# Causal masks added on TensorE: identity and mask tiles in F32R in place of BF16

## The chip, the cores and the metric
The kernel runs as one program on one core of a Trainium2 chip (trn2). The metric is the device time of one launch in microseconds (us); lower is better. A thousand nanoseconds (ns) are one us.

## The reference, cut to what matters
One transformer block for 2048 tokens of width 256: a ternary embedding, a layer norm, an attention of 16 heads with three branches (latent and window branches are causal, the select branch sees 64 chosen tokens), and a mixture of 8 experts.

```python
def _attn(q, k, v, causal):
    scale = 1.0 / math.sqrt(q.shape[-1])
    s = jnp.einsum('bhqd,bhkd->bhqk', q, k) * scale
    if causal:
        mask = jnp.tril(jnp.ones((Tq, Tk), dtype=bool))
        s = jnp.where(mask, s, jnp.finfo(s.dtype).min)
    return jnp.einsum('bhqk,bhkd->bhqd', jax.nn.softmax(s, axis=-1), v)
...
a1 = _attn(q, k1, v1, causal=True)     # latent
a2 = _attn(q, ks, vs, causal=False)    # select
a3 = _attn(q, kw, vw, causal=True)     # window
```

## The kernel before
The program runs in stages: `embed` (weights, tables, constants), `project`, `select`, `attend`, `mix`, `experts`. The change touches constants that `embed` makes, and products in `select` and `attend` that read them.

`attend` takes one head after the other, 16 in all. A head is cut into 84 units. A unit is one block of scores, keys (128 partitions) by up to 512 queries, of one branch. For unit i TensorE (PE) makes the scores with `pe_scores`, and four units later the product with the values with `pe_values`. All these operands are split into an upper and a lower F32R part, so the scores are three products (`three`: upper with upper on L1485, upper with lower on L1488, lower with upper on L1489) and the values two (upper part of the probabilities on L1575, lower on L1577). ScalarE (ACT) takes the exponentials (L1471, L1473), GpSimd (POOL) and VectorE (DVE) make the lower part of the probabilities (L1392). F32R is a 32-bit type that TensorE takes in one pass; the profile prints it as f32 on TensorE.

Between these, `pe_task` puts smaller tasks in the PE's stream, at places that a table (`schedule`) fixes:

- "max": a plain product of queries with keys (L1518), of which VectorE takes the row maxima (L1607). The maxima of the latent branch of this head and of the window branch of the next are made this way. For the select branch it is eight products of 64 columns (L1513).
- "prep": the projections for a later group of four heads (L1485 to L1489 on other tiles, and L1534). The last four heads have none.
- "neg": a transpose of the maxima (L1540).

The task results go to three PSUM banks in turn (`ps_x`, NX = 3), so task n waits until VectorE has read task n - 3.

Where a block of scores lies on the diagonal, the mask is added by a product of its own into the same PSUM bank: the identity is the stationary operand (lhsT) and a 128x128 mask with -1e30 above or below the diagonal is the moving one (rhs). In `pe_scores` this is L1559, between L1485 and L1488; in `pe_task` it is L1521, right behind L1518; in `select` L831, right behind L829. The block before the mask is 512, 384, 256 or 128 columns wide, each as often as the others. The trace writes `out<-moving,stationary`, and takes "ident" for ident16.

All engines run their own instruction streams in order, and the semaphores alone tie them together. The PE's weight loads (LDWEIGHTS, "PEld") are records of their own.

Of the kernel before, what the change touches and what calls it, by code (L numbers as in the profile page):

```python
# [10 lines left out]
F32 = mybir.dt.float32  # L11
F32R = mybir.dt.float32r
BF16 = mybir.dt.bfloat16
I32 = mybir.dt.int32
ALU = mybir.AluOpType
# [3 lines left out]
P = 128  # L19
# [12 lines left out]
MASKED = -1.0e30  # L32
# [57 lines left out]
def embed(nc, g, a, x, weight):  # L90
# [7 lines left out]
    with ExitStack() as ctx:  # L98
# [55 lines left out]
        @block.gpsimd  # L154
        def _(pool):
            pool.dma_start(idx[:], x.rearrange("o (t p) -> p (o t)", p=P)).then_inc(s["idx"], 16)
            cst = Count(pool, s["const"])
            cst.add(nc.gpsimd.memset(g.ones[:], 1.0))
            cst.add(nc.gpsimd.memset(g.ident[:], 0.0))
            cst.wait()  # L160
            cst.add(nc.gpsimd.affine_select(out=g.ident[:], in_=g.ident[:], compare_op=ALU.not_equal, fill=1.0,
                                            base=0, pattern=[[-1, P]], channel_multiplier=1))
            cst.wait()
            cst.add(nc.gpsimd.tensor_copy(g.ident16[:], g.ident[:]))

            cst.add(nc.gpsimd.memset(g.mask_qk[:], 0.0))
            cst.add(nc.gpsimd.memset(g.mask_kq[:], 0.0))
            cst.add(nc.gpsimd.memset(g.strict[:], 1.0))
            cst.add(nc.gpsimd.memset(g.ones16[:], 1.0))
            cst.add(nc.gpsimd.iota(g.slots[:], pattern=[[1, KEEP]], base=0, channel_multiplier=0, allow_small_or_imprecise_dtypes=True))  # L170
            cst.wait()
            cst.add(nc.gpsimd.affine_select(out=g.mask_qk[:], in_=g.mask_qk[:], compare_op=ALU.is_ge, fill=MASKED,
                                            base=0, pattern=[[-1, P]], channel_multiplier=1))
            cst.add(nc.gpsimd.affine_select(out=g.mask_kq[:], in_=g.mask_kq[:], compare_op=ALU.is_ge, fill=MASKED,
                                            base=0, pattern=[[1, P]], channel_multiplier=-1))
            cst.add(nc.gpsimd.affine_select(out=g.strict[:], in_=g.strict[:], compare_op=ALU.is_gt, fill=0.0,
                                            base=0, pattern=[[1, P]], channel_multiplier=-1))
            pool.wait_ge(s["idx"], 16)
            for t in range(NT):
                nc.gpsimd.indirect_dma_start(out=rows[:, t, :], out_offset=None, in_=weight,  # L180
                                             in_offset=bass.IndirectOffsetOnAxis(ap=idx[:, t:t + 1], axis=0)
                                             ).then_inc(s["gather"], 16)
            cst.wait()
            pool.wait_ge(s["wq"], 16 * (1 + KC))
            pool.wait_ge(s["w"], 16 * 6)
            nc.gpsimd.tensor_copy(g.wsm_hi[:], wsm[:]).then_inc(s["whi"], 1)
            nc.gpsimd.tensor_copy(g.wv_hi[:], wvw[:]).then_inc(s["whi"], 1)
            pool.wait_ge(s["whi"], 1)
            nc.gpsimd.tensor_tensor(g.wsm_lo[:], wsm[:], g.wsm_hi[:].bitcast(F32), ALU.subtract).then_inc(s["whi"], 1)
            pool.wait_ge(s["whi"], 2)  # L190
            nc.gpsimd.tensor_tensor(g.wv_lo[:], wvw[:], g.wv_hi[:].bitcast(F32), ALU.subtract).then_inc(s["whi"], 1)
            for n in range(NG):
                k = slot(n)
                if n == 3:
                    pool.wait_ge(wst[k], 32)
                kw = wkw[:, :, n, :]
                nc.gpsimd.tensor_copy(wq_s[k][:, 0, :], wq[:, n, :]).then_inc(s["ws"], 1)
                nc.gpsimd.tensor_copy(wkw_s[k][:, 0], kw).then_inc(s["ws"], 1)
                pool.wait_ge(s["ws"], 4 * n + 1)
                nc.gpsimd.tensor_tensor(wq_s[k][:, 1, :], wq[:, n, :], wq_s[k][:, 0, :].bitcast(F32), ALU.subtract).then_inc(s["ws"], 1)  # L200
                pool.wait_ge(s["ws"], 4 * n + 2)
                nc.gpsimd.tensor_tensor(wkw_s[k][:, 1], kw, wkw_s[k][:, 0].bitcast(F32), ALU.subtract).then_inc(s["ws"], 1)
            pool.wait_ge(s["ws"], 4 * NG)
            pool.wait_ge(s["whi"], 4)
# [532 lines left out]
def select(nc, g, a):  # L737

    with ExitStack() as ctx:
# [75 lines left out]
        @block.tensor  # L815
        def _(pe):
            done = 0

            def max_products(n, last):
                for t, c in maxima[n:last]:  # L820
                    b = bank[6 + n % 2]
                    if n >= 2:
                        pe.wait_ge(s["m_read"], n - 1)
                    if n == 0:
                        pe.wait_ge(s["q"], 48)
                        pe.wait_ge(s["kw"], 48)
                    w = min(CH, (t + 1) * P - c * CH)
                    diag = c == t // 4
                    ins = nc.tensor.matmul(b[:, 0:w], q_hi[0:DQK, t * P:(t + 1) * P], kw_hi[0:DQK, c * CH:c * CH + w], start=True, stop=not diag)  # L829
                    if diag:  # L830
                        ins = nc.tensor.matmul(b[:, w - P:w], g.ident16[:], g.mask_qk[:], start=False, stop=True)  # L831
                    ins.then_inc(s["m"], 1)
                    n += 1
                return n
            pe.wait_ge(s["flag"], 1)
            nc.tensor.matmul(bank[0][:, 0:NT], g.strict[:], flag[:], start=True, stop=False)
            pe.wait_ge(s["run"], 1)
            nc.tensor.matmul(bank[0][:, 0:NT], g.ones[:], run[:], start=False, stop=True).then_inc(s["pos"], 1)
            done = max_products(done, early)
            pe.wait_ge(s["hot"], 1)  # L840
            for kc in range(KC):
                for t in range(NT):
                    last = nc.tensor.matmul(bank[1 + kc][:, 0:KEEP], g.U[:, t, kc * P:(kc + 1) * P], hot[:, t, :], start=(t == 0), stop=(t == NT - 1))
            last.then_inc(s["sel"], 1)
            pe.wait_ge(s["w"], 32)
            pe.wait_ge(s["selc"], 1)
            for n in range(4):
                for kc in range(KC):
                    w = wk[:, kc, n * CH:(n + 1) * CH] if n < 3 else wv[:, kc, :]
                    last = nc.tensor.matmul(bank[(3, 4, 5, 2)[n]][0:KEEP, :], selT[:, kc, :], w, start=(kc == 0), stop=(kc == KC - 1))  # L850
                last.then_inc(s["ks"], 1)
                done = max_products(done, early + (n + 1) * (middle - early) // 4)
            pe.wait_ge(s["rope"], 1)
            for h in range(H):
                last = nc.tensor.transpose(bank[h // 8][0:DQK, (h % 8) * KEEP:(h % 8 + 1) * KEEP], krt[:, h, :], g.ident[0:KEEP, 0:KEEP])
            last.then_inc(s["kt"], 1)
            done = max_products(done, len(maxima))
            pe.wait_ge(s["khi"], 1)
            for n in range(2):
                pe.wait_ge(s["ks_read"], 3)  # L860
                for r in range(8):
                    last = nc.tensor.matmul(bank[3 + n][:, r * KEEP:(r + 1) * KEEP], q_hi[0:DQK, (8 * n + r) * P:(8 * n + r + 1) * P],
                                            khi[0:DQK, 0, 0:KEEP], start=True, stop=True)
                last.then_inc(s["m"], 1)
            pe.wait_ge(s["nm"], 1)
            nc.tensor.transpose(bank[5][0:2 * NT, 0:P], nm[:], g.ident[:]).then_inc(s["turn"], 1)
# [202 lines left out]
def attend(nc, g, a):  # L1069
# [7 lines left out]
    with ExitStack() as ctx:  # L1077
# [418 lines left out]
        def pe_task(pe, t):  # L1496

            n = XN[t]
            bank = ps_x[n % NX]
            if n >= NX:  # L1500
                pe.wait_ge(s["x_read"], n - NX + 1)
            if t[0] == "max":
# [12 lines left out]
                else:  # L1515
# [2 lines left out]
                    last = nc.tensor.matmul(bank[:, 0:w], q_hi[par][0:DQK, q * P:(q + 1) * P], k_hi[b][par][0:DQK, c * CH:c * CH + w],  # L1518
                                            start=True, stop=not diag)
                    if diag:  # L1520
                        last = nc.tensor.matmul(bank[:, w - P:w], g.ident16[:], g.mask_qk[:], start=False, stop=True)  # L1521
            elif t[0] == "prep":
                _, gr, what, j, part = t
                m = NJ * (gr - 1) + j
# [18 lines left out]
        def pe_scores(pe, h, i):  # L1543
# [12 lines left out]
            wait_unit(pe, "p_up", h, i - 3)  # L1556
            qs, ks = slice(j * CH + col, (j + 1) * CH), slice(k * P, (k + 1) * P)
            bank = ps_s[i % 3]
            mid = (lambda: nc.tensor.matmul(bank[:, col:col + P], g.ident16[:], g.mask_kq[:], start=False, stop=False)) if diag else None  # L1559
            aug = DQK + b + 1  # L1560
            three(bank[:, col:CH], k_hi[b][par][0:aug, ks], k_lo[b][par][:, ks], q_hi[par][0:aug, qs], q_lo[par][:, qs], mid, DQK).then_inc(s["scores"], 1)

# [738 lines left out]
def layer(nc, a, out):  # L2301
# [12 lines left out]
    with ExitStack() as ctx:  # L2314
        tile = lambda n, s, d=F32: ctx.enter_context(nc.sbuf_tensor(n, s, d))
        g.ident, g.ones = tile("ident", [P, P]), tile("ones", [P, P])
        g.ident16, g.mask_qk, g.mask_kq = tile("ident16", [P, P], BF16), tile("mask_qk", [P, P], BF16), tile("mask_kq", [P, P], BF16)
        g.gates, g.onehot, g.inv = tile("gates", [P, 3]), tile("onehot", [QA, NB]), tile("inv", [P, 1])
        with ExitStack() as mid:
            with ExitStack() as front:  # L2320
# [84 lines left out]
```

## Time and profile before

| | |
|---|---|
| median of 3 runs | 2747.41 us (2745.13 to 2747.56) |
| the profiled execution | 2745.16 us, span 2743.4 us |
| `attend`, first to last score product | 386.4 to 2312 us of the span |
| TensorE busy | 2327.9 us, 85% of the span |
| VectorE, ScalarE, GpSimd busy | 66%, 64%, 59% |

In the busy times, an instruction's duration runs from start to its modelled end, and two TensorE products that follow each other overlap. For TensorE the distance between the starts of two products is what counts, and it is read from the timeline, whose first column is the start in us and whose second is the duration.

### The profile page before, as it was taken

What the parts mean: (1) busy time and instruction counts of PE and PEld (TensorE: products, weight loads), DVE (VectorE), ACT (ScalarE), POOL (GpSimd) and SP (SyncE); (2) the same over time, 40 slices, a digit from 0 to 9 for tenths busy, and PEclk for the clock granted to TensorE, in tenths of its full rate; (3) what the DMA queues carried; (4) which work ended last, traced back from release to release, by engine and by line L of the source; (5) the groups of instructions that cost most, each with busy time, mean ns of one, the idle gap of its engine ahead of it and who ended that gap; (6) DMA issues with size and microseconds to landing.
All of it is one profiled execution on the core that took longest, in us unless ns stands there. A gap on an engine that the chain in (4) does not pass through costs nothing. (4 is left out here: it accounts for less than half of the span.)

```text
span 2743.4 us, 38402 instructions
## 1 busy us (share of the span) xinstructions
PE 2327.9 (85%) x12402; PEld 1845.8 (67%) x12402; DVE 1815.3 (66%) x2824; ACT 1743.7 (64%) x3574; POOL 1622.2 (59%) x1430
## 2 busy tenths in 40 slices
PE   0178579999999999999999999999999997538885
PEld 0155346777777777777777777777777775538885
DVE  2557457686776868687776868677686773455553
ACT  3433226777777777777777777777778776116663
POOL 4055316667676666767676666766656665006885
PEclk9985569999999999999999999999999998759998
DMA  9757654325151533414251533232132110615776
GB/s 382 311 187 246 189 127 108 91 68 136 24 154 29 136 66 108 112 48 124 52 142 38 138 69 91 61 67 60 34 67 49 32 25 17 194 62 177 197 203 169
DMA packets 199860, 314.87 MB, mean 115 GB/s; under 512 B 95915, under 2 KB 130219, under 8 KB 186731
## 3 DMA queue, kind: packets, MB, share of 16 engines
q1 hardware_dynamic: 189947, 298.23, 37.9%
q0 software_dynamic: 9712, 14.18, 2.8%
q8 instruction: 99, 1.62, 0.3%
q14 instruction: 102, 0.84, 0.1%
HBM read 210.20 MB, written 101.75 MB: 114 GB/s over the span
## 5 line engine op out<-in xcount | busy, mean ns | idle before, releaser
L1392 POOL TENSOR_TENSOR p_lo<-prob,p_hi 128x512 fp32r<-128x512 f32 (+2 forms) x960 | 1092.3, 1145 | 630.0 <-ACT p_hi L1473 544.7
L1471 ACT ACTIVATE prob<-ps_s 128x512 f32<-128x512 f32 (+4 forms) x1344 | 722.8, 538 | 465.8 <-PE ps_s L1489 303.0
L1607 DVE TENSOR_REDUCE max_part<-ps_x 128x1 f32<-128x128 f32 (+1 forms) x1240 | 713.4, 606 | 195.9 <-PE ps_x L1518 128.0
L1473 ACT ACTIVATE p_hi<-ps_s 128x512 fp32r<-128x512 f32 (+3 forms) x1344 | 718.5, 535 | 1.6
L1392 DVE TENSOR_TENSOR p_lo<-prob,p_hi 128x512 fp32r<-128x512 f32 (+1 forms) x320 | 308.0, 962 | 129.8 <-ACT p_hi L1473 124.4
L1575 PE MATMUL ps_o<-p_hi,v_win 128*128 128x512 f32 (+3 forms) x640 | 251.9, 394 | 8.5 <-DVE p_lo L1392 8.5
L1575 PE MATMUL ps_o<-p_hi,v_lat 128*128 128x512 f32 (+3 forms) x640 | 242.6, 379 | 0.0
L1577 PE MATMUL ps_o<-p_lo,v_win 128*128 128x512 f32 (+3 forms) x640 | 234.6, 367 | 0.0
L1577 PE MATMUL ps_o<-p_lo,v_lat 128*128 128x512 f32 (+3 forms) x640 | 234.1, 366 | 0.0
L1668 DVE TENSOR_TENSOR raw_o<-ps_o,low_sum 32x512 f32<-32x512 f32 x192 | 131.4, 684 | 78.9 <-ACT low_sum L1456 74.5
L1518 PE MATMUL ps_x<-k_hi,head_first 96*128 96x512 f32 (+2 forms) x320 | 120.6, 382 | 29.0 <-DVE max_part L1607 28.0
L1518 PE MATMUL ps_x<-k_hi,q_hi 96*128 96x512 f32 (+2 forms) x320 | 120.8, 383 | 26.7 <-DVE max_part L1607 26.0
L1575 PEld LDWEIGHTS ps_o<-p_hi,v_win 128*128 128x128 f32 x640 | 124.1, 194 | 27.3 <-DVE p_lo L1392 13.7
L1577 PEld LDWEIGHTS ps_o<-p_lo,v_lat 128*128 128x128 f32 x640 | 121.8, 190 | 19.6
L1575 PEld LDWEIGHTS ps_o<-p_hi,v_lat 128*128 128x128 f32 x640 | 122.2, 191 | 18.2 <-POOL p_lo L1392 0.3
L1577 PEld LDWEIGHTS ps_o<-p_lo,v_win 128*128 128x128 f32 x640 | 122.5, 191 | 16.8
L1485 PE MATMUL ps_s<-head_first 97*128 97x512 f32 (+1 forms) x320 | 123.5, 386 | 6.1 <-POOL v_lat L1408 6.0
L1488 PE MATMUL ps_s<-head_first 96*128 96x512 f32 (+1 forms) x320 | 128.1, 400 | 0.0
L2127 POOL DMA_INDIRECT xg<-x_scratch,slot_tok x46 | 51.5, 1120 | 128.6 <-POOLq L1723 118.0
L1488 PE MATMUL ps_s<-q_lo,kw_hi 96*128 96x512 f32 (+1 forms) x320 | 126.5, 395 | 0.0
L1488 PE MATMUL ps_s<-q_lo,k_hi 96*128 96x512 f32 (+1 forms) x320 | 126.1, 394 | 0.0
L1488 PE MATMUL ps_s<-head_first,k_hi 96*128 96x512 f32 (+1 forms) x320 | 126.1, 394 | 0.0
(432 smaller groups left out, 5830.9 us busy)
## 6 DMA issues: line engine op xcount, KB each, us to landing
raw<-in_experts_w_dram SPq DMA_DIRECT2D x23, 1536.0 KB
wbuf<-in_tok_weight_dram SPq DMA_DIRECT2D x16, 2000.0 KB, 16.9
head_first<-kw_scratch SPq DMA_DIRECT2D x72, 256.0 KB, 4.7
kw_scratch<-st_hi SPq DMA_DIRECT2D x48, 256.0 KB, 2.8
kw_scratch<-st_lo SPq DMA_DIRECT2D x48, 256.0 KB, 3.3
q_scratch<-st_hi SPq DMA_DIRECT2D x48, 256.0 KB, 4.8
q_scratch<-st_lo SPq DMA_DIRECT2D x48, 256.0 KB, 5.5
head_first<-q_scratch SPq DMA_DIRECT2D x48, 256.0 KB, 7.5
```

The lines of the kernel that those rows point to most:

```text
L1392: ns.tensor_tensor(upper if low else p_lo[:, i % LSLOTS, c:CH], prob[low:P, i % NPROB, c:CH], upper.bitcast(F32), ALU.subtract).then_inc(s ...
L1471: nc.scalar.activation(prob[low:P, i % NPROB, c:CH], ps_s[i % 3][low:P, c:CH], ACT.Exp, scale=SCALE).then_inc(s["p_full"], 1)
L1473: nc.scalar.activation(p_hi[:, i % SLOTS, c:CH], ps_s[i % 3][:, c:CH], ACT.Exp, scale=SCALE).then_inc(s["p_up"], 1)
L1485: nc.tensor.matmul(out, hi, xhi, start=True, stop=False)
L1488: nc.tensor.matmul(out, hi[0:rows] if rows else hi, xlo, start=False, stop=False)
L1518: last = nc.tensor.matmul(bank[:, 0:w], q_hi[par][0:DQK, q * P:(q + 1) * P], k_hi[b][par][0:DQK, c * CH:c * CH + w], start=True, stop=not ...
L1575: last = nc.tensor.matmul(bank[:, c:CH], w, p_hi[:, i % SLOTS, c:CH], start=(k == 0), stop=bool(low))
L1577: last = nc.tensor.matmul(bank[:, c:CH], w, p_lo[:, i % LSLOTS, c:CH], start=False, stop=output_of(i) is not None)
L1607: ins = nc.vector.tensor_reduce(mpart[:, q, c:c + 1], bank[:, 0:w], axis=AX.X, op=ALU.max)
L1668: nc.vector.tensor_tensor(raw_o[j * DV:(j + 1) * DV, h % 2, br, :], ps_o[BANK[out]][DV:2 * DV, :], low_sum[64 * (j % 2):64 * (j % 2) + DV, ...
L2127: nc.gpsimd.indirect_dma_start(out=xg[i % 2][:, q, :], out_offset=None, in_=g.x2_dram, in_offset=bass.IndirectOffsetOnAxis(ap=g.slot_tok[: ...
```

## The change
`ident16` becomes `ident_r`, and it and both masks are F32R in place of BF16. The GpSimd instructions that make them are the same ones on another type (a bitcast is only another view of the same bytes). The PE's stream has the same products in the same places; those on L831, L1521 and L1559 now read two F32R operands. The three tiles take 512 bytes in each partition in place of 256. The order of all instructions on all engines is unchanged.

```diff
@@ embed, gpsimd
-            cst.add(nc.gpsimd.tensor_copy(g.ident16[:], g.ident[:]))
-
-            cst.add(nc.gpsimd.memset(g.mask_qk[:], 0.0))
-            cst.add(nc.gpsimd.memset(g.mask_kq[:], 0.0))
+            cst.add(nc.gpsimd.tensor_copy(g.ident_r[:], g.ident[:]))
+
+            cst.add(nc.gpsimd.memset(g.mask_qk[:].bitcast(F32), 0.0))
+            cst.add(nc.gpsimd.memset(g.mask_kq[:].bitcast(F32), 0.0))
...
-            cst.add(nc.gpsimd.affine_select(out=g.mask_qk[:], in_=g.mask_qk[:], compare_op=ALU.is_ge, fill=MASKED,
+            cst.add(nc.gpsimd.affine_select(out=g.mask_qk[:], in_=g.mask_qk[:].bitcast(F32), compare_op=ALU.is_ge, fill=MASKED,
...
-            cst.add(nc.gpsimd.affine_select(out=g.mask_kq[:], in_=g.mask_kq[:], compare_op=ALU.is_ge, fill=MASKED,
+            cst.add(nc.gpsimd.affine_select(out=g.mask_kq[:], in_=g.mask_kq[:].bitcast(F32), compare_op=ALU.is_ge, fill=MASKED,
@@ select, tensor
-                        ins = nc.tensor.matmul(b[:, w - P:w], g.ident16[:], g.mask_qk[:], start=False, stop=True)
+                        ins = nc.tensor.matmul(b[:, w - P:w], g.ident_r[:], g.mask_qk[:], start=False, stop=True)
@@ attend, pe_task
-                        last = nc.tensor.matmul(bank[:, w - P:w], g.ident16[:], g.mask_qk[:], start=False, stop=True)
+                        last = nc.tensor.matmul(bank[:, w - P:w], g.ident_r[:], g.mask_qk[:], start=False, stop=True)
@@ attend, pe_scores
-            mid = (lambda: nc.tensor.matmul(bank[:, col:col + P], g.ident16[:], g.mask_kq[:], start=False, stop=False)) if diag else None
+            mid = (lambda: nc.tensor.matmul(bank[:, col:col + P], g.ident_r[:], g.mask_kq[:], start=False, stop=False)) if diag else None
@@ layer
-        g.ident16, g.mask_qk, g.mask_kq = tile("ident16", [P, P], BF16), tile("mask_qk", [P, P], BF16), tile("mask_kq", [P, P], BF16)
+        g.ident_r, g.mask_qk, g.mask_kq = (tile(n, [P, P], F32R) for n in ("ident_r", "mask_qk", "mask_kq"))
```

## Rows read from the trace of the kernel before

**Rows 1.** The page: busy us of each engine (share of the span)
```profile
PE 2327.9 (85%) x12402; PEld 1845.8 (67%) x12402; DVE 1815.3 (66%) x2824; ACT 1743.7 (64%) x3574; POOL 1622.2 (59%) x1430
```

**Rows 2.** Head 5 in three windows: length, busy by engine, TensorE's clock, DMA share, GB/s
```profile
1018.20:1030.00 11.80, 11.03 (x60) 8.44 (x59) 9.08 (x14) 8.73 (x19) 10.08 (x9) 1.00 1.02 229
1030.00:1064.20 34.20, 30.56 (x144) 22.41 (x143) 30.21 (x45) 23.64 (x47) 23.91 (x21) 1.00 0.56 170
1064.20:1131.80 67.60, 67.60 (x355) 53.55 (x354) 47.45 (x77) 52.02 (x107) 43.48 (x38) 1.00 0.09 21
```

**Rows 3.** TensorE's waits in head 5 (us in total, times, longest)
```profile
PE ps_x L1518 <- DVE max_part L1607: 3.7, 5, 1.3
```

**Rows 4.** Groups by line: the mask products (busy us, mean ns)
```profile
L1559 PE MATMUL ps_s<-mask_kq,ident 128*128 128x128 bf16 x512 | 119.1, 233 | 0.0
...
L1521 PE MATMUL ps_x<-mask_qk,ident 128*128 128x128 bf16 x496 | 114.9, 232 | 0.0
```

**Rows 5.** Timeline of TensorE, a mask in a block of 512 columns
```profile
1331.15 0.40 PE L1485 MATMUL ps_s<-q_hi,k_hi 99*128 99x512 f32 x1
1331.39 0.23 PE L1559 MATMUL ps_s<-mask_kq,ident 128*128 128x128 bf16 x1
1331.43 0.47 PE L1488 MATMUL ps_s<-q_lo,k_hi 96*128 96x512 f32 x1
1331.75 0.39 PE L1489 MATMUL ps_s<-q_hi,k_lo 96*128 96x512 f32 x1
```

**Rows 6.** Timeline of TensorE, ten products of 512 columns start between these two
```profile
1006.03 0.39 PE L1575 MATMUL ps_o<-p_hi,v_lat 128*128 128x512 f32 x1
...
1008.37 0.40 PE L1575 MATMUL ps_o<-p_hi,v_lat 128*128 128x512 f32 x1
```

**Rows 7.** Timeline of TensorE, a mask (left out) in a block of 256 columns
```profile
1336.65 0.28 PE L1485 MATMUL ps_s<-q_hi,k_hi 99*128 99x256 f32 x1
...
1337.01 0.28 PE L1489 MATMUL ps_s<-q_hi,k_lo 96*128 96x256 f32 x1
```

**Rows 8.** Timeline of TensorE, eight products of 64 columns, then 512
```profile
585.83 0.97 PE L1513 MATMUL ps_x<-ks_hi,head_first 96*128 96x64 f32 x8
586.64 0.48 PE L1575 MATMUL ps_o<-p_hi,v_win 128*128 128x512 f32 x1
586.95 0.40 PE L1577 MATMUL ps_o<-p_lo,v_win 128*128 128x512 f32 x1
```

**Rows 9.** Timeline of TensorE, two products of 128 columns after one of 512
```profile
1334.67 0.23 PE L1575 MATMUL ps_o<-p_hi,v_lat 128*128 128x128 f32 x1
1334.73 0.27 PE L1577 MATMUL ps_o<-p_lo,v_lat 128*128 128x128 f32 x1
1334.85 0.45 PE L1518 MATMUL ps_x<-head_first 96*128 96x512 f32 x1
```

**Rows 10.** Groups of weight loads, 560 to 2180 us (mean ns | idle before, what ended it)
```profile
L1489 PEld LDWEIGHTS ps_s<-head_first 96*128 96x128 f32 x280 | 53.5, 191 | 7.6
...
L1559 PEld LDWEIGHTS ps_s<-mask_kq,ident 128*128 128x128 bf16 x430 | 41.8, 97 | 67.5 <-issue 53.9
```

**Rows 11.** Timeline of TensorE, masks (left out) in blocks of 128 columns
```profile
1338.53 0.22 PE L1518 MATMUL ps_x<-head_first 96*128 96x128 f32 x1
...
1338.94 0.40 PE L1577 MATMUL ps_o<-p_lo,v_lat 128*128 128x512 f32 x1
1339.18 0.23 PE L1485 MATMUL ps_s<-q_hi,k_hi 99*128 99x128 f32 x1
...
1339.43 0.28 PE L1489 MATMUL ps_s<-q_hi,k_lo 96*128 96x128 f32 x1
```

**Rows 12.** Groups by line: GpSimd's gathers, and how it makes masks of either type
```profile
L180 POOL DMA_INDIRECT scratch<-in_tok_weight_dram,tok_idx x16 | 15.3, 959 | 8.7 <-issue 4.6 <-DMA tok_idx<-in_x_dram 4.2
...
L172 POOL TENSOR_SCALAR_AFFINE_SELECT mask_qk<-mask_qk 128x128 bf16<-128x128 bf16 x1 | 0.3, 292 | 0.1
...
L176 POOL TENSOR_SCALAR_AFFINE_SELECT strict<-strict 128x128 f32<-128x128 f32 x1 | 0.3, 286 | 0.0
```

## The prediction
> **What bounds the kernel now.** I read the page first: TensorE is busy for 85% of the span, no other engine for more than 66% [rows 1]. Then the windows of one head of the attention. In its last 67.6 us TensorE is busy for all 67.6 us, with VectorE at 47.45 and ScalarE at 52.02, and the clock is at its full level of 2.4 GHz, 1.00 [rows 2]. Here TensorE alone sets the pace: every ns that its stream gains or loses is a ns of the run. In the 46 us before, 1018.2 to 1064.2, TensorE is busy 41.59 us and VectorE 39.29 us [rows 2], and TensorE's waits, 3.7 us in five pieces, are all of one kind: a "max" product on L1518 waits for VectorE to have read the bank of three tasks ago [rows 3]. In this stretch a shorter TensorE stream mostly makes those waits longer. The order of the streams is unchanged, so what remains is the price of one mask product, and there are 512 on L1559 and 496 on L1521 [rows 4]; a quarter of each stand behind a block of 512, 384, 256 and 128 columns.
>
> **What a mask costs now.** The recorded durations (233 ns, rows 4) overlap with their neighbours, so I go by starts. From L1485 to L1489 of a diagonal block with 512 columns it is 1331.75 - 1331.15 = 0.60 us [rows 5]. Ten starts of 512-column products take 2.34 us, 0.234 each [rows 6], so that two of them would take 0.468, and the mask adds 0.132. With 256 columns the same distance is 0.36 [rows 7]; at half of 0.234 a product, two would take 0.234, and the mask adds 0.126. The mask itself starts L1488 only 0.04 us after it, but L1488 then lasts 0.47 and holds L1489 back to 0.32 [rows 5]: the wait is for L1488's weights, not for the mask's stream.
>
> **What an F32R product costs that is shorter than its weight load.** Eight F32R products of 64 columns and the start of the next take 0.81 us, and that next one, 512 wide, then takes 0.31 to the start behind it in place of 0.234 [rows 8]. Both come out of one rule: a product can't begin to stream until about 0.111 us after the one before began, because its weights load meanwhile. A record starts when the product before has finished streaming (64 columns: 0.03), so the first distance is 0.03 and seven are 0.111: 0.03 + 0.78 = 0.81. The last begins 0.111 - 0.03 = 0.08 after its record and streams 0.234: 0.31. Two 128-column F32R products say the same: the first distance is 0.06 (the stream), the second 0.12 [rows 9]. So F32R streams 128 columns in 0.06, at the same rate as 512, and no short block pays more than its weight load.
>
> **Why the BF16 mask costs 0.132 and not 0.111.** The weight load of an F32R product starts with the product before; that of the mask doesn't. Its group shows 53.9 us of idle time before it with no cause but "issue", for 430 loads [rows 10], where the loads of L1489 show none by that name. So now a mask pays some 0.02 for its own load, late and short, and then 0.111 for the load of the F32R product behind it.
>
> **The sum, by width.** I take it that the F32R mask is treated as the F32R products of rows 8 and 9 are.
> - Block of 512, 384 or 256 columns: the mask's load of 0.111 hides under the product before, which streams 0.117 or more. The mask starts on time, and the product behind it streams 0.111 later. The mask adds 0.111 in place of 0.126 to 0.132: -0.015 to -0.021, I take -0.018. There are 384 + 372 = 756 of them: -13.6 us.
> - Block of 128 columns: the product before streams only 0.06, so that the mask now waits for its own load too. On L1559, L1485 to L1489 is now 1339.43 - 1339.18 = 0.25 [rows 11] and becomes 0.06 + 0.111 + 0.111 = 0.282: +0.032, 128 times: +4.1 us. On L1521 with a 512-column product behind, it is now 1338.94 - 1338.53 = 0.41 [rows 11] and becomes 0.06 + 0.111 + (0.051 + 0.234) = 0.456: +0.045 by this instance, 124 times. The narrow block pays for the same wait as on L1559, and a timeline gives a difference to no better than 0.01, so between +0.032 and +0.045 I take +0.037: +4.6 us.
>
> All masks of the attention: -13.6 + 4.1 + 4.6 = -4.9 us, about -0.31 a head. How much of it counts: by a count in the timeline of head 5, 22 of its 64 masks start in the stretch from 1018.2 to 1064.2. By width they are 8 on L1559 (two of each) and 14 on L1521 (four each of 128 and 256, three each of 512 and 384), which comes to 16 x -0.018 + 2 x 0.032 + 4 x 0.037 = -0.076 us. If all of that disappears in VectorE's waits, a head is left with -0.23 and the run with -3.7 us; if none, -4.9. The last four heads have no prep tasks and fewer such waits. I take -4 us. Against the profiled execution (2745.16) this is 2741; that execution is 2.25 us below the median of the runs, and against the median the forecast is 2747.4 - 4 = 2743.4 us.
>
> **The rest of the edit at nothing.** GpSimd makes a mask in 292 ns as BF16 and in 286 as F32 [rows 12], and afterwards it waits 4.2 us for the token indices before the gathers on L180 [rows 12], which covers some 0.1 us either way. Without that cover it would be 0.1 us. The 16 masks of `select` (L831) at some 0.02 to 0.1 each are between -0.4 and +1 us. The larger tiles move the addresses of those behind them; no row prices that, and I take nothing, with a bound of 1 us either way.
>
> **A rule against the change.** Rows 10 show 97 ns for a BF16 load and 191 for an F32R one. The Trainium skill, "TensorE: Matmul & The Clock Gate", section "Weight-path perf modes — Fast Weight Load (FWL) and DoubleRow", says that a full 128-column load that isn't FP32 is read in a faster mode with four chunks at once, and that FP32 gains nothing there. The trace agrees as to the order of the two. By that page alone the change gives up a faster load on every mask, and the estimate from its P / 1.2 ns for a plain load is 107 ns against a quarter of it, 80 ns more for each of 1008 masks, or +81 us. This is a price only where the load is exposed.
>
> **Rivals.**
> 1. *The mask's load stays exposed* (slower). The idle time before the mask's load could come from something other than its type: from the identity being reused, or from a product that adds into the bank that is being written. Then the F32R load of 0.111 stands open before each mask, and the mask adds 0.111 + 0.111 = 0.222 in place of 0.132: +0.09 each. Times 1008 that is +91 us, or with the 22 of 64 masks in the VectorE-bound stretch counted at nothing, +60: 2807 to 2838 us. It decides from the point where the load is late by more than 0.02. Against it: L1488 adds into the bank that L1485 writes and its load is early. For it: no row shows this load in F32R. 6%.
> 2. *The 128-column blocks lose nothing* (clearly faster). If the load of the identity could start before the product in front of it, or were shorter, only the -0.018 would be left, times 1008: -18 us, 2729. Rows 8 and 9 speak against it, with 128 stationary columns in each. 7%.
> 3. *Nothing measurable, gain and loss cancel.* If a third of the 0.018 belongs to the short product and not to its type, the wide masks give 756 x -0.012 = -9.1, the narrow ones +8.7: 2747. 25%.
> 4. *The losses weigh more.* If an F32R mask behind a wide product is no cheaper at all (the late load was hidden too, and 0.132 is what any short product costs there), the narrow ones stand alone: +8.7 us, less the VectorE-bound part, 2753 to 2756. Rows 8 speak against it (0.31 in place of 0.32 behind the short product). 10%.
> 5. The forecast above, from -2 to -7 us: 52%.
>
> **How the numbers follow.** The likeliest is 2743.4 us, its own range 2740 to 2746. The range for 8 in 10 takes rivals 3 and part of 4 in and leaves 1 and most of 2 out: 2733 to 2751. What a measurement of this kernel can tell from no change is about 0.2%, 5.5 us. The forecast's range reaches over that line with a third of its weight or somewhat more, 0.20 of 0.52; with rival 2 and a little of rival 3 that is 0.30 for faster. Slower is rivals 1 and most of 4, 0.13. The rest, 0.57, is no change.
>
> **What would show it.** In the changed profile the loads on L1559 and L1521 should last about 190 ns and have no "issue" before them; from L1485 to L1489 it should be 0.58 us with 512 columns (0.60 now), 0.345 with 256 (0.36) and 0.28 with 128 (0.25). The three windows of rows 2, 113.6 us together, should become 113.4. If the load still starts with the mask and L1485 to L1489 takes 0.69, rival 1 holds. If L1559 shows a distance of more than 0.06 to the next start behind a wide block, an F32R mask streams more slowly than rows 9 let expect, and the sum is wrong there.

## The result and the profile after

The changed kernel takes 2751.01 us (median of 16 runs) against 2746.15 us before (16 runs): ratio 1.0025, 95% interval 1.0016 to 1.0035. That is slower and not 4 us faster: by some 7 us going by the ratio and the means of the 16 runs (2752.5 against 2745.4), by 4.9 us going by the medians. The range of the prediction ended at 2751.0. Ratios leave out two executions in the runs further down, one of run 4 (3343 us) and one of the kernel before beside runs 5, 8, 9 and 11 (3344 us), which had a granted clock of 0.65 where all others have 0.93.

The profiled execution of the changed kernel took 2754.81 us, with a span of 2753.1 us. Of the 9.6 us between the two profiled spans, 0.5 lie ahead of the attention, 2.6 in its first head and 0.3 behind the last. The first head has no weight in this: over the thirteen kernels profiled here it took from 126.5 to 137.7 us, in no order by kernel. What is left, 6.3 us, comes from heads 1 to 15: 5.4 from heads 1 to 14 and 0.9 from the last. Up to head 14 it is regular: heads 1 to 11 take 122.81 us (from the first L1485 of one to that of the next) where they took 122.39, all but head 10, which takes 122.23; heads 12 to 14, which have no prep tasks, take 0.44 to 0.47 us more than before.

**The products themselves.** The timeline of TensorE in the changed kernel, a mask behind blocks of 512, 256 and 128 columns:

```profile
1091.57 0.40 PE L1485 MATMUL ps_s<-q_hi,k_hi 99*128 99x512 f32 x1
1091.81 0.22 PE L1559 MATMUL ps_s<-mask_kq,ident_r 128*128 128x128 f32 x1
1091.87 0.44 PE L1488 MATMUL ps_s<-q_lo,k_hi 96*128 96x512 f32 x1
1092.15 0.39 PE L1489 MATMUL ps_s<-q_hi,k_lo 96*128 96x512 f32 x1
...
1017.33 0.29 PE L1485 MATMUL ps_s<-q_hi,kw_hi 97*128 97x256 f32 x1
...
1017.69 0.28 PE L1489 MATMUL ps_s<-q_hi,head_first 96*128 96x256 f32 x1
...
1018.28 0.23 PE L1485 MATMUL ps_s<-q_hi,kw_hi 97*128 97x128 f32 x1
1018.34 0.27 PE L1559 MATMUL ps_s<-mask_kq,ident_r 128*128 128x128 f32 x1
1018.45 0.27 PE L1488 MATMUL ps_s<-q_lo,kw_hi 96*128 96x128 f32 x1
1018.56 0.28 PE L1489 MATMUL ps_s<-q_hi,head_first 96*128 96x128 f32 x1
```

The rows show 0.58 us from L1485 to L1489 with 512 columns, where [rows 5] have 0.60, and 0.28 with 128, where [rows 11] have 0.25. The mask streams for 0.06 us and L1488 for 0.28 behind it; behind the narrow block the distances are 0.06, 0.11 and 0.11. This is the model of the prediction to within 0.01 us. The medians over all such blocks of heads 2 to 14 (start distances, 104 of each) are 0.576, 0.468, 0.352 and 0.285 us for 512, 384, 256 and 128 columns, and in the kernel before 0.598, 0.484, 0.367 and 0.249.

The weight loads, as groups in the stretch 560 to 2180 us:

```profile
L1559 PEld LDWEIGHTS ps_s<-mask_kq,ident_r 128*128 128x128 f32 x428 | 81.5, 190 | 13.4
L1521 PEld LDWEIGHTS ps_x<-mask_qk,ident_r 128*128 128x128 f32 x429 | 81.1, 189 | 11.9
```

They last 190 ns in place of 97 [rows 10], and the idle time "issue" in front of them is gone. The load of the mask at 1091.81 starts at 1091.57, with L1485; in [rows 5] it starts with its own product, at 1331.39.

**Where the time went.** TensorE's waits from 600 to 2200 us. First the changed kernel, then the kernel before:

```profile
PE ps_x L1518 <- DVE max_part L1607: 42.7, 59, 1.4
PE ps_o L1575 <- DVE p_lo L1392: 7.6, 13, 0.6
PE ps_x L1540 <- DVE neg_max L1611: 5.0, 12, 0.4
```

```profile
PE ps_x L1518 <- DVE max_part L1607: 42.6, 59, 1.3
PE ps_o L1575 <- DVE p_lo L1392: 7.5, 13, 0.6
```

A wait stands there that wasn't there before: the transpose of the negated row maxima (L1540, unit 40 of a head) waits for VectorE's L1611, 0.42 us as a record, once a head. The same place in the timeline of the changed kernel, head 5, TensorE, VectorE and GpSimd:

```profile
1078.44 0.40 PE L1489 MATMUL ps_s<-q_hi,head_first 96*128 96x512 f32 x1
1079.26 0.27 PE L1540 MATMUL ps_x<-ident,neg_max 128*16 128x128 f32 x1 [0.42 <-DVE neg_max L1611]
...
1075.69 1.30 POOL L1392 TENSOR_TENSOR p_lo<-prob,p_hi 128x512 fp32r<-128x512 f32 x1 [0.17 <-ACT p_hi L1473]
1075.72 1.82 DVE L1691 TENSOR_TENSOR raw_o<-raw_o 128x512 f32<-128x512 f32 x1
1077.57 1.29 DVE L1607 TENSOR_REDUCE max_part<-ps_x 128x1 f32<-128x512 f32 x2
1078.89 0.22 DVE L1611 TENSOR_REDUCE neg_max<-max_part 128x16 f32<-128x64 f32 x1
```

and of the kernel before:

```profile
1070.98 0.69 DVE L1691 TENSOR_TENSOR raw_o<-raw_o 128x512 f32<-128x512 f32 x1
1071.00 1.81 POOL L1392 TENSOR_TENSOR p_lo<-prob,p_hi 128x512 fp32r<-128x512 f32 x1 [0.22 <-ACT p_hi L1473]
```

L1691 is the last addition of the three branches' outputs of the head before, which VectorE does in unit 35. It lasts 1.82 us in place of 0.69, and GpSimd's subtraction of unit 36 lasts 1.30 in place of 1.81. Before, VectorE starts 0.02 us ahead of GpSimd; after, GpSimd starts 0.03 us ahead. Whoever is first runs at its own length, and the other lasts 1.12 us (VectorE) or 0.5 us (GpSimd) longer. VectorE is then 1.12 us late for L1607 and L1611. L1489 to L1540 takes 0.82 us in place of 0.233, so TensorE stands for 0.58 us of it; the other 0.54 it had in hand. (The 0.42 of the record is the idle time from the end of L1489's record, which is 0.40 long and would overlap the next one.) Head 10, where GpSimd comes 0.19 us behind VectorE in both kernels, has no such wait, and it alone is shorter than before.

### The profile page after: what moved, and what is told of

Same layout as the page of the kernel before. It is cut to its first block and busy times, and to the rows that moved or that the text cites. A ratio compares the mean times of both kernels' runs of the same rounds, so it can differ in the third digit from the quotient of the medians.

```text
span 2753.1 us, 38402 instructions
## 1 busy us (share of the span) xinstructions
PE 2335.7 (85%) x12402; PEld 1963.3 (71%) x12402; DVE 1838.7 (67%) x2824; ACT 1744.1 (63%) x3574; POOL 1607.8 (58%) x1430
## 5 line engine op out<-in xcount | busy, mean ns | idle before, releaser
L1392 POOL TENSOR_TENSOR p_lo<-prob,p_hi 128x512 fp32r<-128x512 f32 (+2 forms) x960 | 1080.3, 1134 | 650.9 <-ACT p_hi L1473 566.0
L1607 DVE TENSOR_REDUCE max_part<-ps_x 128x1 f32<-128x128 f32 (+1 forms) x1240 | 714.7, 606 | 196.6 <-PE ps_x L1518 126.7
L1575 PE MATMUL ps_o<-p_hi,v_win 128*128 128x512 f32 (+3 forms) x640 | 246.3, 385 | 8.7 <-DVE p_lo L1392 8.7
L1575 PE MATMUL ps_o<-p_hi,v_lat 128*128 128x512 f32 (+3 forms) x640 | 239.5, 374 | 0.0
L1575 PEld LDWEIGHTS ps_o<-p_hi,v_win 128*128 128x128 f32 x640 | 122.2, 191 | 28.1 <-DVE p_lo L1392 13.9
L1575 PEld LDWEIGHTS ps_o<-p_hi,v_lat 128*128 128x128 f32 x640 | 120.9, 189 | 18.6 <-POOL p_lo L1392 0.3
L1485 PE MATMUL ps_s<-head_first 97*128 97x512 f32 (+1 forms) x320 | 122.8, 384 | 6.3 <-POOL v_lat L1408 6.0
L1488 PE MATMUL ps_s<-head_first 96*128 96x512 f32 (+1 forms) x320 | 124.6, 389 | 0.0
L1488 PE MATMUL ps_s<-q_lo,kw_hi 96*128 96x512 f32 (+1 forms) x320 | 122.2, 382 | 0.0
L1488 PE MATMUL ps_s<-q_lo,k_hi 96*128 96x512 f32 (+1 forms) x320 | 122.0, 381 | 0.0
L1488 PE MATMUL ps_s<-head_first,k_hi 96*128 96x512 f32 (+1 forms) x320 | 122.0, 381 | 0.0
```

The lines of the kernel that those rows point to most:

```text
L1392: ns.tensor_tensor(upper if low else p_lo[:, i % LSLOTS, c:CH], prob[low:P, i % NPROB, c:CH], upper.bitcast(F32), ALU.subtract).then_inc(s ...
L1485: nc.tensor.matmul(out, hi, xhi, start=True, stop=False)
L1488: nc.tensor.matmul(out, hi[0:rows] if rows else hi, xlo, start=False, stop=False)
L1575: last = nc.tensor.matmul(bank[:, c:CH], w, p_hi[:, i % SLOTS, c:CH], start=(k == 0), stop=bool(low))
L1607: ins = nc.vector.tensor_reduce(mpart[:, q, c:c + 1], bank[:, 0:w], axis=AX.X, op=ALU.max)
```

## The experiments

Theory A: the F32R masks shorten TensorE's stream as forecast, but bring GpSimd's subtraction forward past VectorE's addition, and the 0.58 us wait a head comes from that. Theory B: F32R masks themselves cost time. A head below is the median length of heads 1 to 11 in the profiled execution. Most heads of a profile repeat to some 0.1 us or better, so this is the finer measure; the ratio of whole runs carries the unsteady first head. Every ratio is to the kernel before.

**1. VectorE late by a memset, BF16 masks.**

```diff
                 if br == 2:
                     dve.wait_ge(s["done"], 2 * h + 1)
+                    nc.vector.memset(tick[:, 0:32], 0.0)
```

> The kernel before (BF16 masks) with one added VectorE memset of 128x32 in front of the last addition of each head's output (L1691, third branch), so that this addition starts some 0.05 to 0.15 us later. Theory A (the changed kernel is slower because the addition now starts just behind GpSimd's subtraction of unit 36 in place of just ahead of it): the addition lasts 1.8 us in place of 0.69, the transpose L1540 waits about 0.6 us, a head takes 122.9 to 123.0 us in place of 122.4, and the run is 7 to 10 us slower (ratio 1.0025 to 1.0035) with not one F32R mask in it. Theory B (the F32R masks themselves cost the time, in TensorE's stream or its clock): no change, within 1 us.

Measured: ratio 0.9996 (0.9984 to 1.0008), head 122.37, the addition 0.65 us. The two engines in head 5:

```profile
1069.58 1.81 POOL L1393 TENSOR_TENSOR p_lo<-prob,p_hi 128x512 fp32r<-128x512 f32 x1 [0.22 <-ACT p_hi L1474]
1069.60 0.09 DVE L1692 MEMSET tick<- 128x32 f32 x1
1069.60 0.66 DVE L1693 TENSOR_TENSOR raw_o<-raw_o 128x512 f32<-128x512 f32 x1
```

As theory B had it, but the edit didn't do what it was for. By the record starts the addition is now 6 to 19 ns behind GpSimd (15 in head 5, all heads but head 10), and yet it is GpSimd that waited (1.81 us). So the outcome of the pair did not flip, and this run tells nothing between A and B. Why VectorE stayed the first isn't shown. It does show that the order of two record starts this close is not always the order that counts. Run 5 makes the delay in another way.

**2. GpSimd late, F32R masks.** One more instruction on GpSimd, behind the waits of unit 36 and in front of its subtraction.

```diff
+            if i == 36:
+                nc.gpsimd.memset(tick[:], 0.0)
```

> The changed kernel (F32R masks) with one added GpSimd memset of 128x128 between the waits and the subtraction of unit 36, so that this subtraction starts some 0.14 us later and VectorE's addition is ahead of it again. Theory A: the addition is back at 0.69 us, L1540 waits for nothing, a head takes 122.2 us, and the run is 2 to 4 us faster than the kernel before (ratio 0.9985 to 0.9993), 8 to 10 faster than the changed one. Theory B: as slow as the changed kernel, ratio 1.0025.

Measured: ratio 0.9984 (0.9971 to 0.9998), head 122.23. All additions are short again (the source line of the addition; least, median and greatest ns of the 32):

```profile
L1694 DVE TENSOR_TENSOR raw_o<-raw_o x32: 683/692/693, 574.2 to 2324.5; 128x512 f32<-128x512 f32 x32
```

With an instruction more than the changed kernel, this one is faster by more than 0.5 us a head. Theory B falls as the cause of the slowdown.

**3 and 4. The addition moved out of the way, with F32R and with BF16 masks.**

```diff
-        FINISH = {20: 0, 27: 1, 29: 2, 31: 3, 33: 4, 35: 5}
+        FINISH = {20: 0, 27: 1, 29: 2, 31: 3, 33: 4, 37: 5}
```

> The changed kernel with the last step of the output (L1691, third branch) moved from unit 35 to unit 37, behind the last row maximum and its negation L1611. Theory A: the addition finds GpSimd idle (between its units 36 and 39) and stays near 0.69 us, and the transpose no longer hangs on it in any case: no wait on L1540, a head of 122.2 us, ratio to the kernel before 0.998 to 0.9993. Theory B: ratio 1.0025.

> The kernel before with the same move of the last step to unit 37. Theory A: TensorE had no wait there, so nothing is won: ratio 0.9995 to 1.0003, a head of 122.4 us. With after_fin37 it then gives what the F32R masks are worth alone: my sum says 3 to 5 us in the whole run.

Measured: with F32R 0.9985 (0.9971 to 1.0000), head 122.23; with BF16 0.9995 (0.9981 to 1.0008), head 122.41. Without the collision the F32R masks are worth 0.18 us a head, some 2.8 us in 16 heads. That is the sign of the forecast, and less than its 4 us. But it doesn't come from where the forecast had it. The sum of the prediction, cut by units, against the medians of heads 1 to 11 from run 4 to run 3:

| stretch of a head | length | masks wide, narrow | forecast | measured |
|---|---|---|---|---|
| units 0 to 6 | 8.7 us | 4, 1 | -0.04 | -0.03 |
| units 7 to 32, the waits for VectorE | 46.0 us | 16, 6 | 0, at most -0.08 | -0.06 |
| units 33 to 40 | 10.5 us | 4, 0 | -0.07 | -0.11 |
| units 41 to 83, TensorE alone | 57.2 us | 24, 9 | -0.12 | +0.02 |

So the whole gain is made ahead of unit 41. Behind it, taken from the start of the product in front of a mask to the start of the second one behind it, the 24 wide masks gain 0.345 us, 0.014 each, and the nine narrow ones lose 0.35: 0.034 to 0.039 each, and 0.10 for two that stand next to each other. The two cancel, but for 0.02.

**5. VectorE late by a read of PSUM, BF16 masks.** `longer` is true for the last row maximum of unit 35.

```diff
+                    if longer:
+                        nc.vector.tensor_reduce(tick[:, 8 * h + q % 8:8 * h + q % 8 + 1], bank[:, 0:32], axis=AX.X, op=ALU.max)
                     ins = nc.vector.tensor_reduce(mpart[:, q, c:c + 1], bank[:, 0:w], axis=AX.X, op=ALU.max)
```

> The kernel before (BF16 masks) with one added VectorE row maximum of 32 columns of a PSUM bank, into a tile that nobody reads, once a head in unit 35, so that the addition L1691 of the third branch starts about 0.1 us later and behind GpSimd's subtraction of unit 36. It reads PSUM, where the memset of the run before_dve_late wrote SBUF and was itself ahead of GpSimd. Theory A (which of the two starts first decides): the addition lasts 1.7 to 1.8 us in place of 0.69, GpSimd's subtraction 1.3 in place of 1.8, L1540 waits 0.5 to 0.7 us, a head takes 122.9 to 123.1 in place of 122.4, the run is 7 to 10 us slower than the kernel before (ratio 1.0025 to 1.0037). Theory B (the F32R masks cost the time by themselves): 0.1 us a head at most, ratio 1.0000 to 1.0006.

Measured: ratio 1.0024 (1.0013 to 1.0035), head 122.87. The timeline of VectorE:

```profile
1071.97 0.18 DVE L1609 TENSOR_REDUCE tick<-ps_x 128x1 f32<-128x32 f32 x1
1072.07 0.68 DVE L1610 TENSOR_REDUCE max_part<-ps_x 128x1 f32<-128x512 f32 x1
1072.78 0.69 DVE L1671 TENSOR_TENSOR raw_o<-ps_o,low_sum 32x512 f32<-32x512 f32 x1
1073.50 1.77 DVE L1694 TENSOR_TENSOR raw_o<-raw_o 128x512 f32<-128x512 f32 x1
```

The added instruction puts VectorE 0.10 us back. The addition is then 0.07 us behind GpSimd and lasts 1.77 us, and L1540 waits 0.35 us as a record, less than expected. The head is 0.48 us longer than before and the ratio that of the changed kernel: the whole slowdown, without one F32R mask.

**6 and 7. Half of the masks.** F32R for L1559 alone, and for L1521 alone; the select stage stays BF16.

> F32R masks only in the score blocks (L1559, mask_kq); those of the row maxima (L1521) and of the select stage stay BF16; order of the steps as before. Behind TensorE's last wait for VectorE in a head (unit 32) exactly one mask of each kind runs before ScalarE releases GpSimd's subtraction of unit 36 (both in unit 34, both behind 384 columns). Each moves that subtraction 0.02 us forward against the addition L1691, from 0.02 behind it to level with it; both moved it to 0.03 ahead. Theory A: level is too close to call; if the addition wins (0.69 us) a head is 122.3 us and the ratio 0.999, if it loses (1.8 us) a head is 122.9 us and the ratio 1.0025. Either way duration and head go together. Without theory A a head should be half of the change's way in both runs.

> The other half: F32R masks only in the row maxima (L1521), BF16 in the score blocks. The same expectation: one mask in unit 34 moves GpSimd's subtraction 0.02 us forward, level with the addition; 122.3 us a head and a ratio of 0.999 where the addition stays at 0.69, 122.9 and 1.0025 where it lasts 1.8.

Measured: L1559 alone 1.0016 (1.0005 to 1.0027), head 122.77, GpSimd 0.011 to 0.020 us ahead (a shift of about 0.04 us and not the expected 0.02), and all additions but that of head 10 long. L1521 alone 0.9997 (0.9987 to 1.0006), and here the heads of one execution fall apart. VectorE and GpSimd in head 1, then in head 2:

```profile
581.94 1.84 DVE L1698 TENSOR_TENSOR raw_o<-raw_o 128x512 f32<-128x512 f32 x1
...
581.93 1.30 POOL L1399 TENSOR_TENSOR p_lo<-prob,p_hi 128x512 fp32r<-128x512 f32 x1 [0.19 <-ACT p_hi L1480]
...
704.75 0.69 DVE L1698 TENSOR_TENSOR raw_o<-raw_o 128x512 f32<-128x512 f32 x1
...
704.75 1.84 POOL L1399 TENSOR_TENSOR p_lo<-prob,p_hi 128x512 fp32r<-128x512 f32 x1 [0.20 <-ACT p_hi L1480]
```

Of heads 1 to 14, the five in which GpSimd starts 6 to 9 ns ahead have an addition of 1.83 us (and those of the first twelve heads take 122.79 to 122.84 us). The eight in which the distance is between 2 ns ahead and 1 ns behind, and head 10 with 185 ns behind, have one of 0.69 us (122.23 to 122.25). Up to the start of unit 40 the eleven heads agree to 0.03 us (63.82 to 63.85); from there they take 58.97 to 58.99 with a long addition and 58.40 with a short one. So duration and head go together, in one execution of one kernel, as theory A has it.

**8. F32R only behind the narrow blocks.** Order of the steps as before.

> The mirror image: F32R masks only behind blocks of 128 columns, BF16 behind the others, order of the steps as before. By my sum each narrow mask costs 0.032 (L1559) or 0.037 us (L1521), 8 of each a head, less those in VectorE's stretch: +0.35 to +0.55 us a head (122.75 to 122.9), +6 to +8 us in the run by TensorE's stream alone. Theory A also says that TensorE and ScalarE are then later and not earlier against VectorE, so that the addition L1691 stays ahead of GpSimd (0.69 us) and L1540 doesn't wait.

Measured: ratio 1.0027 (1.0015 to 1.0040), head 122.69, or +0.30; the additions last 0.69 us and L1540 doesn't wait. The mechanism is as expected; the size is below the expected 0.35 to 0.55. The heads account for some 5 us of the 7.5 that the ratio gives. The profiled execution (2747.68 us) is 5.8 us below the median of its runs, and where the rest is stays open.

**9, 10 and 11. F32R only behind the wide blocks,** with the addition in unit 37, with it in unit 35, and with the first multiplication (L1685; in the kernel before it lasts 1.78 us in heads 1 to 15, 1.65 in head 8) moved as well. The choice is made where the product is issued:

```diff
-    g.ident_r[:], g.mask_qk[:]
+    (g.ident16 if w == P else g.ident_r)[:], (g.mask_qk16 if w == P else g.mask_qk)[:]
...
-    g.ident_r[:], g.mask_kq[:]
+    (g.ident16 if col == 3 * P else g.ident_r)[:], (g.mask_kq16 if col == 3 * P else g.mask_kq)[:]
```

> F32R masks behind blocks of 512, 384 and 256 columns, BF16 masks behind blocks of 128 (and in the select stage), and the last addition in unit 37 as in after_fin37. By my sum the wide masks alone are worth -0.018 us each, 47 a head, less what VectorE's waits swallow (16 of them): -0.55 us a head against the kernel before (122.4 to 121.8), -9 us in the run, ratio 0.9965 to 0.9975; after_fin37 has 122.23. Against it: if BF16 and F32R loads side by side cost something at each change, it is no better than after_fin37.

> F32R masks behind blocks of 512, 384 and 256 columns as in wide_fin37, but the last addition stays in unit 35. Theory A: both masks of unit 34 are F32R, GpSimd is ahead, the addition lasts 1.8 us and L1540 waits: of the 0.6 us a head that wide_fin37 won, nearly all is given back, a head takes 122.3 to 122.5 us, ratio 0.999 to 1.001.

> As wide_fin37, and the first multiplication of the output (L1685, first branch), which lasts 1.78 us in every head of every kernel so far where it needs about 0.69, moves from unit 27 to unit 28, behind two row maxima, where GpSimd has just finished a subtraction and waits about 1.1 us for the next. Theory A: it lasts 0.68 to 0.97, and as VectorE sets the pace there, nearly all of the 0.8 to 1.1 us comes off the head: 120.7 to 121.1 us in place of 121.8, 2720 to 2726 us in all (ratio 0.990 to 0.992). If it meets GpSimd there too, nothing is won over wide_fin37.

Measured: with the addition in unit 37 0.9966 (0.9953 to 0.9979), head 121.81, which is 0.60 below the BF16 kernel with the same move. With it in unit 35 0.9989 (0.9979 to 0.9998), head 122.36: the collision is back (1.81 us), and takes 0.55 of the 0.60. With the multiplication in unit 28 0.9894 (0.9872 to 0.9916; 2716.78 us median), head 120.63. The timeline of VectorE and GpSimd there:

```profile
1049.91 1.18 DVE L1692 TENSOR_TENSOR raw_o<-raw_o,o_weight 128x512 f32<-128x512 f32 x1
...
1049.24 1.29 POOL L1399 TENSOR_TENSOR p_lo<-prob,p_hi 128x512 fp32r<-128x512 f32 x1 [1.80 <-ACT p_hi L1480]
```

GpSimd still has 0.62 us to go when it begins, not none, so that it lasts 1.18 us and not 0.69 to 0.97. But TensorE's waits for VectorE fall from 43.3 us to 27.3 (600 to 2200 us, some 13 heads), 1.2 us a head, and that is the whole gain, more than the 0.8 to 1.1 expected. The multiplication is only 0.60 us shorter. The move also takes it from in front of two row maxima to behind them, and TensorE waits for such maxima; how much of the 1.2 us is the collision and how much the new place isn't shown. First with the multiplication in unit 27, then in unit 28:

```profile
PE ps_x L1525 <- DVE max_part L1614: 43.3, 59, 1.3
...
PE ps_x L1525 <- DVE max_part L1614: 27.3, 55, 0.8
```

## Why the prediction was wrong, step by step

- *What an F32R mask costs, the load of the mask under a wide block and the wait behind a narrow one*: right. 0.58 us (forecast 0.58) with 512 columns, 0.352 (0.345) with 256, 0.285 (0.28) with 128, loads of 190 ns without the idle time. Rival 1 (load exposed, 0.69) and rival 2 (narrow blocks free) are out. So is the price given under "A rule against the change", 80 ns for each mask: by the records an F32R load lasts 93 ns longer (190 against 97), and behind a wide block none of it is paid.
- *The sum by width*: right in sign, too large. The flat -0.018 is -0.022, -0.016 and -0.015 on L1559 for 512, 384 and 256 columns by the medians, but -0.014 over all wide masks of the last stretch, and a narrow one there costs 0.039 and not 0.034. So where TensorE alone sets the pace the masks give +0.02 us a head and not -0.12, which is what rival 3's -0.012 for a wide mask gives. Run 3 against run 4 gives -0.18 us a head where the sum had -0.23 to -0.31. That it comes that near is in part luck: the gain lies ahead of that stretch.
- *The step that failed* is "How much of it counts", with its premise "In this stretch a shorter TensorE stream mostly makes those waits longer". A shift of the stream against VectorE was priced between nothing and its own size, -0.076 us, and a loss by it was given no bound. The waits took little of it (-0.06 of the -0.076 came through), and just behind the stretch the shift brought a loss of 0.58 us. I counted what TensorE could gain, and not whom a shift of the others' starts would bring into whose way. (The stretch also has a wait of another kind, which I left out: L1575 waits 0.6 us once for VectorE's p_lo.) TensorE's last wait in the stretch (unit 32) ties it to VectorE; behind that, two wide masks in unit 34 bring GpSimd's subtraction, which follows ScalarE, some 0.05 us forward against VectorE. VectorE's addition was 0.02 us ahead. The price is +0.58 us in 14 heads, 8.1 us, against a gain of 2.8. The difference, 5.3 us, lies between the 4.9 of the medians and the 7 of the ratio.
- None of the five rivals had the collision. Rival 4 gave the right size (2753 to 2756) for another reason, which the medians refute: a wide mask is cheaper in F32R. The check that I named for a wrong prediction, the starts around the masks, would have found nothing; it is the list of TensorE's waits that shows it, by a line that is new.
- The collision could be read from the kernel before. Its timeline has GpSimd's subtraction at 1.81 us beside most others of 1.28, starting 0.02 us behind VectorE's addition; that a swap would cost VectorE 1.1 us is what L1685 shows, 1.78 us where it starts 0.06 us behind GpSimd. The Trainium skill, "SBUF — State Buffer", section "🔬 SBUF: two separate sides", says that VectorE and GpSimd share one pair of ports as an exclusive lock: a VectorE instruction with two SBUF inputs and a GpSimd one that reads SBUF don't overlap, and whichever "starts first gets the pair for the whole instruction". The runs agree: 0.69 and 1.81 us one way, 1.30 and 1.82 the other, and the same swap from one head to the next in run 7. Only run 1 doesn't fit by its record starts, as said there.

## What to carry to other kernels

Before costing a small shift at its own size, list the pairs of two-input SBUF instructions of VectorE and GpSimd that start within some 0.1 us of each other, and ask who waits for the loser: here 0.05 us decided over 0.58 us a head. Compare the lists of waits of the two traces first: here one new line there told more than all durations around the masks. Here a 128-column product between F32R products costs its neighbour's weight load (0.11 us) and not its stream (0.06), so choose its type by what it lies between: F32R behind wide blocks, BF16 behind narrow ones gave 0.60 us a head, where F32R for all gave 0.18.

## What the runs showed that I had not expected

- The tie is sharp within one kernel. GpSimd 6 ns ahead by the records: VectorE loses; 2 ns ahead: VectorE wins (run 7). It is no rule for all kernels: with the memset of run 1 VectorE wins with GpSimd up to 19 ns ahead. In run 5 the addition is 0.07 us behind and lasts 1.77 us, which is what GpSimd still has to go plus 0.55; the same sum gives 1.82 in the changed kernel and 1.17 (measured 1.18) in run 11.
- A GpSimd memset didn't hold VectorE up. In run 2 it starts 0.03 to 0.04 us ahead of the addition (but in head 10) and lasts 0.21, and the addition still takes 0.69 us.
- Moving L1685 by one unit was worth 1.2 us a head, more than all the mask types together: 0.9966 to 0.9894 with one number in `FINISH`.
